# Snapshots copied ahead of the splits they stood beside, and two matrix sums in one VectorE instruction

## What is computed

```python
xn = _layernorm(x)
K = _s4_kernel(Lambda, p, q, B, Ct, step, L)
y = irfft(rfft(xn, n=2*L) * rfft(K, n=2*L), n=2*L)[..., :L] + D[0] * xn
Wg, Wu, Wd = (dequantize(w, scale, zero) for each)   # (nibble - zero) * scale
g = xn @ Wg.T                 # inter = 2752
u = xn @ Wu.T
out = x + y + (silu(g) * u) @ Wd.T
```

## Time and profile before

| | |
|---|---|
| median of 3 runs | 1354.57 us (1353.21 to 1356.82) |
| profiled execution, its own time | 1356.75 us |
| its span, first to last instruction | 1354.9 us |
| TensorE busy | 1305.4 us, 96% |
| VectorE busy | 921.3 us, 68% |
| ScalarE busy | 460.8 us, 34% |
| GpSimd busy | 670.9 us, 50% |
| mean granted TensorE clock | 0.993 |

### The profile page before, as it was taken

How to read it: one execution, slowest core, us unless ns; L and a number is a source line. 1 busy time by engine, 2 the same in 40 slices (tenths; PEclk the granted TensorE clock), 3 DMA queues, 4 the chain that set the end, 5 groups by cost and what they waited for, 6 DMA issues and landing times.

```text
span 1354.9 us, 16976 instructions
## 1 busy us (share of the span) xinstructions
PE 1305.4 (96%) x6303; PEld 621.8 (46%) x6303; DVE 921.3 (68%) x1008; ACT 460.8 (34%) x815; POOL 670.9 (50%) x484
## 2 busy tenths in 40 slices
PE   3799899999999999999999999899999999999999
PEld 2454344444444444444444444344444444444444
DVE  7886898979899989999897877334424323242331
ACT  5664454554454545444554544310000000000000
POOL 6785877878787887777787867510000000000000
PEclk9899999999999999999999999999999999999999
DMA  9304455545546454544544545999283344436331
GB/s 315 86 1 131 133 148 164 155 149 163 156 133 194 133 178 140 179 132 143 175 150 148 155 139 161 391 387 323 77 263 101 101 173 153 117 101 225 102 101 62
DMA packets 165455, 218.08 MB, mean 161 GB/s; under 512 B 42236, under 2 KB 122750, under 8 KB 163454
## 3 DMA queue, kind: packets, MB, share of 16 engines
q1 hardware_dynamic: 163934, 200.69, 47.5%
q10 hardware_dynamic: 1440, 16.32, 3.0%
HBM read 139.64 MB, written 77.34 MB: 160 GB/s over the span
## 4 chain that ended last, share of the span: by engine, by line
PE 73%; DVE 8%; issue 2%; ACT 1%; POOL 1%; DMA 0%; SPq 0%; ACTq 0%; DVEq 0%
PE px L1403 22%; PE px L1490 17%; PE pz L1403 11%; PE pz L1490 8%; PE pv L1517 6%; PE py L1403 5%; PE py L1490 4%; DVE wf L1575 2%; DVE wf L1572 1%; DVE wf L1576 1%; DVE hf L1705 0%; DMA w_d<-ds 0%; POOL ds L723 0%; DVE hf L1708 0%; DVE wf L1649 0%
## 5 line engine op out<-in xcount | busy, mean ns | idle before, releaser
L1403 PE MATMUL px<-xo,wo 128*128 128x512 f16 x2016 | 461.6, 382 | 15.1 <-ACT u L1038 10.9
L1403 PEld LDWEIGHTS px<-xo,wo 128*128 128x128 f16 x2016 | 197.7, 99 | 256.5 <-issue 9.7
L714 POOL TENSOR_TENSOR wo<-wf,wo 128x512 f16<-128x512 f32 x147 | 235.9, 1615 | 60.6 <-ACT wo L982 60.4
L733 POOL TENSOR_TENSOR hs<-hf,hs 128x512 f16<-128x512 f32 x154 | 204.8, 1336 | 87.0 <-ACT hs L1019 84.7
L1403 PE MATMUL pz<-xo,wo 128*128 128x512 f16 x1008 | 232.6, 381 | 2.8 <-POOL wo L714 2.5
L1490 PE MATMUL px<-wd,hr 128*128 128x512 f16 x1056 | 232.3, 379 | 0.0
L1490 PEld LDWEIGHTS px<-wd,hr 128*128 128x128 f16 x1056 | 102.3, 98 | 118.7 <-issue 0.2
L1403 PEld LDWEIGHTS pz<-xo,wo 128*128 128x128 f16 x1008 | 98.8, 98 | 122.3 <-DVE xo L1564 3.1
L982 ACT ACTIVATE wo<-wf 128x512 f16<-128x512 f32 x147 | 90.9, 621 | 91.5 <-DVE wf L1576 80.4
L1575 DVE TENSOR_TENSOR wf<-wf,sz 128x1024 f32<-128x1024 int32 x63 | 117.0, 1858 | 4.7 <-DMA sz<-in_sz_gate 1.5
L1490 PE MATMUL pz<-wd,hr 128*128 128x512 f16 x528 | 116.6, 379 | 0.0
(11 more groups left out here) (220 smaller groups left out, 1405.3 us busy)
## 6 DMA issues: line engine op xcount, KB each, us to landing
h_d<-hs SPq DMA_DIRECT2D x154, 256.0 KB, 2.5
hr<-h_d SPq DMA_DIRECT2D x56, 704.0 KB, 4.3
w_d<-ds SPq DMA_DIRECT2D x73, 256.0 KB, 2.0
wd<-w_d ACTq DMA_DIRECT2D x4, 2816.0 KB, 15.8
sz<-in_sz_gate SPq DMA_DIRECT2D x21, 512.0 KB, 5.2
sz<-in_sz_up SPq DMA_DIRECT2D x21, 512.0 KB, 4.9
sz<-in_sz_down SPq DMA_DIRECT2D x20, 512.0 KB, 5.1
xc_d<-xo SPq DMA_DIRECT2D x8, 1024.0 KB, 7.6
```

The lines of the kernel that those rows point to most:

```text
L714: pool.tensor_tensor(w_dest(t, j, 1), w_place_of(j), w_dest(t, j, 0), ALU.subtract).then_inc(wlo_done, 1)
L733: pool.tensor_tensor(hs[:, j, :, 1, :], h_place_of(p, j), hs[:, j, :, 0, :], ALU.subtract)\
L1403: done = pe.matmul(bank[:, :], wo[t % 2][:, j, wp, k * P:(k + 1) * P], xo[p][:, j, xp, k, :], start=(j in (0, 3) and k == 0 and wp == 0 an ...
```

## The change

Four things. (1) The sign of S3 and of T3 is turned, for x and for h and for both kinds of weights, so that S3 T3 is the same; S2 adds S3 where it subtracted it. (2) T1 and T3 now have the form B12 minus something, and one VectorE instruction of 128x1024 makes both, with B12 broadcast; likewise for down weights. (3) S1 and S2 of h both add A22, and one instruction of 128x1024 makes both. The semaphores count one less for each. (4) In ScalarE's list snap_s5 stands ahead of the split of B11 and snap_u2 ahead of that of B21 in units 4g and 4g+2; and snap_s1(43) ahead of the splits of S1 and S2 of the last tile's first half.

```diff
-T_ORDER = (T1, T3, T2, T4)
-T_POS = {j: i for i, j in enumerate(T_ORDER)}
+T_ORDER = (T1, T2, T4)
+T_POS = {T1: 0, T3: 0, T2: 1, T4: 2}
...
-              x0, x1, op = {S1: (a21, a22, ALU.add), S3: (a11, a21, ALU.subtract),
-                            S2: (a22, x_sum(q, S3), ALU.subtract), S4: (a12, x_sum(q, S2), ALU.subtract)}[j]
+              x0, x1, op = {S1: (a21, a22, ALU.add), S3: (a21, a11, ALU.subtract),
+                            S2: (a22, x_sum(q, S3), ALU.add), S4: (a12, x_sum(q, S2), ALU.subtract)}[j]
...
                up_nibble(2 * g + 1)
                h_high(g - 1, 1, A12)
                d_high(g - 1, T1)
+               snap_s5(n)
                w_high(2 * g + 1, B11)
-               snap_s5(n)
                scale_angles(n)
                h_high(g - 1, 1, A22)
+               snap_u2(n)
                w_high(2 * g + 1, B21)
-               snap_u2(n)
                silu_first(n)
...
                up_nibble(2 * g + 2)
+               snap_s5(n + 2)
                w_high(2 * g + 2, B11)
-               snap_s5(n + 2)
                scale_angles(n + 2)
+               snap_u2(n + 2)
                w_high(2 * g + 2, B21)
                d_high(g, B21)
-               snap_u2(n + 2)
...
            silu_tail(42)
+
+           snap_s1(43)
            h_high(NG, 0, S1)
            h_high(NG, 0, S2)
-
-           snap_s1(43)
...
                if j == T1:
                    dve.wait_ge(deq_done, slab_up(t) + 1)
                    dve.wait_ge(wlo_done, base + W_POS[B11] + 1)
-                   dve.tensor_tensor(b11, b12, b11, ALU.subtract).then_inc(wsum_done, 1)
-               if j == T3:
-                   dve.tensor_tensor(b12, b22, b12, ALU.subtract).then_inc(wsum_done, 1)
+                   blocks = wf[:, :, :, :, :].rearrange("p s m n w -> p (s m n w)")[:, 0:10 * 256]\
+                       .rearrange("p (a b w) -> p a b w", a=2, b=5)
+                   dve.tensor_tensor(wf[:, 0, :, :, 0:256], wf[:, 0, 1:2, :, 0:256].broadcast_to((P, 2, 2, 256)),
+                                     blocks[:, :, 0:3:2, :], ALU.subtract).then_inc(wsum_done, 1)
...
-                   dve.tensor_tensor(b11, b12, b11, ALU.subtract).then_inc(dsum_done, 1)
-               if j == T3:
                    if g == NG:
                        dve.wait_ge(wzero_done, 1)
-                   dve.tensor_tensor(b12, b22, b12, ALU.subtract).then_inc(dsum_done, 1)
+                   k = 0 if g == NG else 1
+                   blocks = wf[:, :, :, :, :].rearrange("p s m n w -> p (s m n) w")
+                   dve.tensor_tensor(wf[:, k, :, 0, :], wf[:, k, 1:2, 0, :].broadcast_to((P, 2, 512)),
+                                     blocks[:, 4 * k:4 * k + 4:3, :], ALU.subtract).then_inc(dsum_done, 1)
...
-               dve.tensor_tensor(a, a, hf[p][:, 0, 1, :], ALU.subtract).then_inc(hs3_done, 1)
+               dve.tensor_tensor(a, hf[p][:, 0, 1, :], a, ALU.subtract).then_inc(hs3_done, 1)
...
-               dve.tensor_tensor(a21, a21, a22, ALU.add).then_inc(hsum_done, 1)
                dve.wait_ge(hs3_done, q + 1)
                dve.wait_ge(elo_done, 2 * q + 2)
-               dve.tensor_tensor(a, a22, a, ALU.subtract).then_inc(hsum_done, 1)
+
+               dve.tensor_tensor(hf[p][:, 0, :, :], hf[p][:, 0, :, :], hf[p][:, 1, 1:2, :].broadcast_to((P, 2, SB)),
+                                 ALU.add).then_inc(hsum_done, 1)
```

More of the change, by code:

```diff
@@ L151, in sum_place @@
 def sum_place(g, j):
-    return 4 * g + T_POS[j]
+    return 3 * g + T_POS[j]
 def slab_arrived(m):
@@ L742, in h_zero @@
                 pool.wait_ge(llo_done, 5 * (2 * (NG - 1) + p) + 5)
-                pool.wait_ge(hsum_done, 3 * (2 * (NG - 1) + p) + 3)
+                pool.wait_ge(hsum_done, 2 * (2 * (NG - 1) + p) + 2)
                 pool.memset(hf[p][0:P - TB, 1, :, :], 0.0).then_inc(hzero_done, 1)
@@ L976, in w_high @@
                 if j in T_POS:
-                    act.wait_ge(wsum_done, 4 * t + T_POS[j] + 1)
+                    act.wait_ge(wsum_done, 3 * t + T_POS[j] + 1)
                 else:
@@ L985, in v_high @@
                 if j == 2:
-                    act.wait_ge(wsum_done, 4 * 21 + 1)
+                    act.wait_ge(wsum_done, 3 * 21 + 1)
                 else:
@@ L1009, in h_high @@
                 elif j in (S1, S2, S4):
-                    act.wait_ge(hsum_done, 3 * (2 * g + p) + (S1, S2, S4).index(j) + 1)
+                    act.wait_ge(hsum_done, 2 * (2 * g + p) + (2 if j == S4 else 1))
                 else:
@@ L1620, in t_sum @@
                     dve.wait_ge(wlo_done, base + W_POS[B11] + 1)
-                    dve.tensor_tensor(b11, b12, b11, ALU.subtract).then_inc(wsum_done, 1)
-                if j == T3:
-                    dve.tensor_tensor(b12, b22, b12, ALU.subtract).then_inc(wsum_done, 1)
+                    blocks = wf[:, :, :, :, :].rearrange("p s m n w -> p (s m n w)")[:, 0:10 * 256]\
+                        .rearrange("p (a b w) -> p a b w", a=2, b=5)
+                    dve.tensor_tensor(wf[:, 0, :, :, 0:256], wf[:, 0, 1:2, :, 0:256].broadcast_to((P, 2, 2, 256)),
+                                      blocks[:, :, 0:3:2, :], ALU.subtract).then_inc(wsum_done, 1)
                 if j == T2:
                     dve.wait_ge(wlo_done, base + W_POS[B22] + 1)
-                    dve.wait_ge(wsum_done, 4 * t + 1)
+                    dve.wait_ge(wsum_done, 3 * t + 1)
                     dve.tensor_tensor(b22, b22, b11, ALU.subtract).then_inc(wsum_done, 1)
                 if j == T4:
-                    dve.wait_ge(wsum_done, 4 * t + 3)
+                    dve.wait_ge(wsum_done, 3 * t + 2)
                     dve.tensor_tensor(b21, b21, b22, ALU.subtract).then_inc(wsum_done, 1)
@@ L1700, in h_s12 @@
                 n = max(unit(2 * g, p), unit(2 * g + 1, p))
-                a, a21, a22 = hf[p][:, 0, 0, :], hf[p][:, 0, 1, :], hf[p][:, 1, 1, :]
                 dve.wait_ge(hf_done, 2 * n + 2)
@@ L1712, in h_s4 @@
                 dve.wait_ge(llo_done, 5 * q + L_POS[A12] + 1)
-                dve.wait_ge(hsum_done, 3 * q + 2)
+                dve.wait_ge(hsum_done, 2 * q + 1)
                 a12 = hf[p][:, 1, 0, :]
@@ L1888, in _ @@
             t_sum(0, T1)
-            t_sum(0, T3)
             for b in range(15, 18):
@@ L1902, in _ @@
             t_sum(1, T1)
-            t_sum(1, T3)
             x_stats(5)
@@ L1935, in _ @@
             t_sum(2, T1)
-            t_sum(2, T3)
             t_sum(2, T2)
@@ L1941, in _ @@
             d_sum(0, T1)
-            d_sum(0, T3)
             h_first(3, 1, 1)
@@ L1953, in _ @@
                 t_sum(2 * g + 1, T1)
-                t_sum(2 * g + 1, T3)
                 s4_work(n)
@@ L1972, in _ @@
                 t_sum(2 * g + 2, T1)
-                t_sum(2 * g + 2, T3)
                 h_s3(g, 1)
@@ L1984, in _ @@
                 d_sum(g, T1)
-                d_sum(g, T3)
                 h_s4(g, 0)
```

## The result

| | before | changed |
|---|---|---|
| median of 20 runs | 1355.99 us | 1364.9 us |
| lowest to highest | 1352.86 to 1372.21 | 1356.47 to 1371.84 |
| profiled execution | 1356.75 us | 1371.84 us |
| its span | 1354.9 us | 1370.0 us |

The ratio of the times is 1.005, 95% interval 1.0029 to 1.0072. The forecast was 1345.3 us, so it had the wrong sign. The kernel before lies near 1354 in most executions, but in 8 of these 20 it lies above 1362; the changed one lies above 1360 in 18 of 20. In what follows the spread is therefore as telling as the median.

The account below looks back on a forecast made before the run. With TensorE busy 1305.4 of 1354.9 us, only its idle and lower-clock time could be won. The terms summed to -9.3 us, taking the profiled 1356.75 to 1347.5 and the median 1354.57 to 1345.3; range 1341 to 1350.5.

Parts of the forecast that it names:

- the whole down projection: nothing: Down projection, after the projection: the change was costed at no effect there, its length staying as before.
- slower rival: GpSimd lacks room, B21's split waits 1.3 us at 18 places: +14 us, 1368 us; chance 0.04.
- waits for landings between 870 and 900: Around the projection's end: listed as a sign that the forecast was wrong, with no size given.
- the end's step: End of the projection, stall at 857.95: snap_s1(43) starts earlier, but snap_u3 still waits for a store's landing; -1.7 us.
- 136: Stall at 136.21 us: T1 comes 0.54 later, so +0.54 us, bounds 0 and +2.3; 3.5 us idle expected.
- 158: Stall at 158.36 us: shrinks to 1.6 us idle with no lower clock, -3.9 us, bounds -2.2 and -5.5.
- 197: Stall at 197.68 us: snap_u2 starts at 192.6 instead of 196.96, -1.0 us, bounds 0 and -1.2.
- short ones: Three short stalls, one at 381.48, behind snap_u2 or VectorE's h: -1.3 us, bounds 0 and -1.3.
- 619: Stall at 619.91 us: three merged loaded pairs save VectorE about 2.9 us, so -1.9 us, bounds 0 and -1.9.
- 857: Stall at 857.95 us, projection's end: snap_s1(43) no longer waits behind S1 and S2; -1.7 us, bounds -1.3 and -3.7.
- the rival in which it falls: The first stall, 3.5 us at 136, trips the lower clock: 1347.0 us; chance 0.12.
- the price of a merged instruction: VectorE's merged 128x1024 instructions: 2.06 us each beside GpSimd, 1.22 us free of it.

Follow-up runs that it names:

- e3: The changed kernel plus a ScalarE wait for the landing of hr_in[3] ahead of the loads of wd3 and wd4: median 1353.8 us, ratio 0.995.
- e4: The kernel before plus a ScalarE wait for the landing of hr_in[3] ahead of the loads of wd3 and wd4: median 1354.9 us, ratio 0.996.
- e17: The same kernel as e4, timed again in another group of runs: median 1356.4 us, ratio 0.999.
- e10: The kernel before with only the merged instructions and signs, no reordered copies, plus the wait of e4: median 1357.0 us, ratio 0.999.
- e14: The kernel of e3 with the copy snap_u2(3) alone moved ahead of w_high(2, T1): median 1349.4 us, ratio 0.994.

## Why the prediction was wrong, step by step

**The step that failed** is "the whole down projection: nothing". It costed the landings behind the end of the projection at nothing, and its slower rival was put at GpSimd, which had the room that was said. The list of signs had it ("waits for landings between 870 and 900"), without a price or a chance. The rows to price it were there: the end's step took a store's landing of 7.0 us and the queue's being full as given, and did not ask what TensorE's earlier finish would start: 5632 KB of loads of wd3 and wd4 by ScalarE, all in packets 44 times as large as the stores' 512 bytes (the loads of acc aside). In the profiled execution this is 15.0 us idle and 1.9 us of lower clock behind it (16.27 for 66 matmuls; 14.40 in e3), and 0.68 idle more within the first term, at 877.85.

**The rest of the sum** was -9.3 and came to about -1.8. Term by term, idle time and clock, in the profiled execution:

| place | forecast | found |
|---|---|---|
| 136 | +0.5 | +3.1: 3.52 idle (forecast 3.5), and 5.30 instead of 2.76 for the twelve matmuls |
| 158 | -3.9 | -4.6: 0.98 idle, no lower clock |
| 197 | -1.0 | +3.2: gone there, but 2.77 idle and 1.7 of clock at 191.5 |
| short ones | -1.3 | -1.3 |
| 619 | -1.9 | -0.25 |
| 857 | -1.7 | -2.0: 1.10, 1.41, 1.09 idle (forecast 0.4, 1.5, 1.9) |

From the issue of hr, which marks the projection's end, less the start of the first stall, it is 737.9 us against 739.6, so -1.7, which agrees.

*136.* The idle time was right. That the clock would stay full behind it was wrong; the rival in which it falls had 0.12. In seven profiles with 3.5 us there the clock fell each time (12 matmuls in 4.12 to 5.30). It also fell after 2.98, in six of the seven profiles with the old instructions (4.05 to 5.30); the one of before, on which the step rested, is the exception. The 1.69 us of lower clock that the sum counted as won at 158 is no firmer: behind the same idle time the twelve matmuls took 2.75 in e4 (3.85 idle) and in e17 (3.84), the two in which the first stall had cost 5.30. Nor is that at 857: after 4.01 in e17 they took 2.76. One execution can't say where the clock falls.

*197.* The arithmetic of the copies was right, the place was not. VectorE does the S4 kernel's small steps there, and its h is what ScalarE stands at. B11's split, at 193.71 in the earlier trace rows and forecast for 190.9, came at 194.54. Here is ScalarE in the changed kernel at the split of h ahead of that; before, this split began at 189.42 after a wait of 2.70:

```profile
190.25 0.63 ACT L1020 ACTIVATE hs<-hf 128x512 f16<-128x512 f32 x1 [6.08 <-DVE hf L1676]
190.79 0.58 ACT L1027 ACTIVATE py<-px 128x512 f32<-128x512 f32 x1
```

snap_s1(6) stands behind this split of h, and h comes from VectorE. Counted from the start of the first stall (131.96 and, before, 133.23), TensorE came to this wait 1.3 us sooner than before and h 2.1 us later (56.8 against 58.1, 58.3 against 56.2). Two things made h late. The first stall with its lower clock held VectorE too, by 3.3 us. And from its first step behind it (L1662 at 143.60, L1657 at 141.60 before) to h (L1676 at 189.53, L1671 at 188.70), VectorE took 45.9 us instead of 47.1: 1.2 us saved by three merged pairs, where the forecast had 3.3. The rows say where the rest went. T2's and T4's place of the down weights, changed, then before:

```profile
155.61 1.64 DVE L1654 TENSOR_TENSOR wf<-wf 128x512 f32<-128x512 f32 x1
157.28 1.53 DVE L1657 TENSOR_TENSOR wf<-wf 128x512 f32<-128x512 f32 x1
```

```profile
155.47 0.68 DVE L1649 TENSOR_TENSOR wf<-wf 128x512 f32<-128x512 f32 x1
156.18 0.69 DVE L1652 TENSOR_TENSOR wf<-wf 128x512 f32<-128x512 f32 x1
```

Two instructions that ran free of GpSimd now run beside it: 1.8 us given back at one place.

*619.* The merged instructions had the price that was forecast: means of 2.09, 1.67 and 1.30 us (the last two partly beside an idle GpSimd; forecast 2.06 loaded, 1.22 free). The earlier trace rows stand for before.

```profile
L1712 DVE TENSOR_TENSOR hf<-hf 128x1024 f32<-128x1024 f32 x22 | 45.9, 2086 | 3.1 <-POOL hs L734 3.1
L1625 DVE TENSOR_TENSOR wf<-wf 128x1024 f32<-128x1024 f32 x21 | 35.1, 1670 | 0.6
L1649 DVE TENSOR_TENSOR wf<-wf 128x1024 f32<-128x1024 f32 x11 | 14.3, 1300 | 0.1
```

The time did not stay won here either. Ahead of 619 the third instruction behind S1 with S2's, the last of the dequantizing, which had run free of GpSimd in 1.22 us before (at 606.20), now met it, 2.17, and the 0.95 between them is most of what S1 with S2 had saved:

```profile
598.39 2.17 DVE L1712 TENSOR_TENSOR hf<-hf 128x1024 f32<-128x1024 f32 x1
600.49 1.37 DVE L1573 TENSOR_SCALAR wf<-raw 128x512 int32<-128x512 int32 x1
601.89 2.06 DVE L1576 TENSOR_TENSOR wf<-wf,sz 128x1024 f32<-128x1024 int32 x1
603.99 2.17 DVE L1577 SCALAR_TENSOR_TENSOR wf<-wf,sz 128x1024 f32<-128x1024 f32 x1
606.20 1.23 DVE L1625 TENSOR_TENSOR wf<-wf 128x1024 f32<-128x1024 f32 x1
```

Overall this line (L1577, before L1576) went from 1816 to 1938 ns on average, GpSimd's additions at L739 from 1465 (L738) to 1599. The step left out that with one collision fewer GpSimd's work does not vanish: it meets the next instruction. The Trainium skill, SBUF — State Buffer, section "Who interferes with whom", states that a VectorE instruction with two SBUF inputs contends with a GpSimd instruction that reads SBUF, and calls the shared port pair an exclusive lock. These rows agree: 1.22 us free of GpSimd, 2.17 beside it.

**What was right**: the price of a merged instruction, 158 to 0.7 us, and the end's three stalls in place and sum (3.6 against 3.8). **What stays open**: whether the mergers alone lose anything (e10 against e4 and e17: 2.1 and 0.6 us); how much of hr's delay is the packet size and how much the time at which the loads began; and how far e14's 4.4 us over e3 is the clock alone, since each kernel left one profile.

## What to carry over

Where a change lets an engine finish a stage sooner, list the transfers that this finish starts, and what is still queued on the other queues at that time, before costing the next stage at nothing. A small, urgent transfer shares the DMA engines with a large one packet by packet, so its packet size decides its share: hold the large load back by a wait on the landing of the urgent one. And when most runs of a kernel agree and a third lie 10 us higher, look for a race in the one trace before building on its rows.
